# Layer 3's weight tables in float32r from high and low parts, with a reordered prologue

## What is computed

```python
x = x + conv1d(x, W, groups=4, taps=9, pad=4) + (cond @ c_weight.T + bias)[:, :, None]
for n in (1, 2, 3):
    h = gelu(cond @ W0 + b0); h = gelu(h @ W1 + b1)
    att = softmax(h @ W2 + b2)                       # 8 weights per sample
    agg_w = einsum('bk,koi->boi', att, weight)       # a 64x64 matrix per sample
    x = x + einsum('boi,bih->boh', agg_w, x) + (att @ bias_k)[:, :, None]
```

## Time and profile before

| what | value |
|---|---|
| median of three runs | 327.9 us |
| the profiled execution | 329.1 us |
| its span in the trace | 327.3 us |
| PE busy | 317.1 us (97%), 1479 instructions |
| PEld busy | 256.4 us (78%) |
| DVE busy | 253.0 us (77%) |
| ACT busy | 227.6 us (70%) |
| POOL busy | 158.8 us (49%) |
| DMA | 104.80 MB, 320 GB/s on average |

### The profile page before, as it was taken

One profiled execution on the slowest core, in us unless ns is written; L12 is line 12 of the kernel. 1 busy time (PEld: TensorE's weight loads), 2 busy tenths in 40 slices (PEclk: granted clock), 3 DMA queues, 4 the chain that ended last, 5 costly groups with the idle time before them and its releaser, 6 DMA issues.

```text
span 327.3 us, 5950 instructions
## 1 busy us (share of the span) xinstructions
PE 317.1 (97%) x1479; PEld 256.4 (78%) x1479; DVE 253.0 (77%) x231; ACT 227.6 (70%) x344; POOL 158.8 (49%) x269
## 2 busy tenths in 40 slices
PE   8899999999999999999999999999999999999993
PEld 8787868888888787688788887777888887888862
DVE  4593968788886886977888867788788878887674
ACT  5445597777777778776767777787777676777662
POOL 8001289887444454545544445555555454444500
PEclk9999999999999999999999999999999999999999
DMA  7994356998999999989998999998999999897658
GB/s 255 262 289 172 132 208 222 356 375 354 349 332 348 362 334 364 345 322 359 371 355 335 339 338 354 336 373 340 341 365 366 346 357 365 320 353 291 267 212 340
DMA packets 29948, 104.80 MB, mean 320 GB/s; under 512 B 3353, under 2 KB 3609, under 8 KB 21978
## 3 DMA queue, kind: packets, MB, share of 16 engines
q1 hardware_dynamic: 29940, 104.70, 86.2%
HBM read 36.53 MB, written 33.55 MB: 214 GB/s over the span
## 4 chain that ended last, share of the span: by engine, by line
PE 76%; DMA 8%; issue 6%; DVE 6%; ACT 2%; POOL 1%; DVEq 0%; POOLq 0%
PE bank L394 43%; PE bank L430 8%; DMA ybuf<-conv_sb 8%; PE bank L432 7%; PE bank L431 7%; PE bank L402 4%; PE bank L509 2%; DVE mix_lo L739 1%; ACT conv_sb L594 1%; PE bank L438 1%; PE bank L451 1%; POOL a_dup L359 1%; DVE ybuf L729 1%; DVE x_lo L715 1%; ACT x_hi L587 1%
## 5 line engine op out<-in xcount | busy, mean ns | idle before, releaser
L349 POOL COPY a_diag<-table 64x64 f32 (+1 forms) x128 | 87.7, 685 | 117.6 <-PE bank L402 85.1
L594 ACT ACTIVATE conv_sb<-bank 128x512 f32<-128x512 f32 x128 | 76.6, 598 | 70.6 <-PE bank L394 66.3
L715 DVE TENSOR_TENSOR x_lo<-x_sb,x_hi 128x2064 fp32r<-128x2064 f32 x32 | 74.0, 2312 | 41.6 <-ACT x_hi L587 40.4
L394 PE MATMUL bank<-x_hi,toep_hi 128*128 128x512 f32 x256 | 84.5, 412 | 0.0
L394 PE MATMUL bank<-x_lo,toep_hi 128*128 128x512 f32 x256 | 80.7, 397 | 0.0
L394 PE MATMUL bank<-x_hi,toep_lo 128*128 128x512 f32 x256 | 80.5, 396 | 0.0
L359 POOL COPY a_dup<-table 64x128 f32 (+1 forms) x128 | 64.4, 503 | 30.8 <-DVE table L803 13.2
L729 DVE TENSOR_TENSOR ybuf<-ybuf 128x2048 fp32r<-128x2048 f32 x31 | 72.1, 2324 | 1.7 <-ACT ybuf L598 1.6
L614 ACT ACTIVATE out_sb<-bank,beta 128x512 f32<-128x512 f32 x93 | 63.7, 687 | 4.6 <-PE bank L432 1.6
L587 ACT ACTIVATE x_hi<-x_sb 128x2064 fp32r<-128x2064 f32 x32 | 61.6, 1924 | 3.1 <-DMA x_sb<-in_x 2.9
L394 PEld LDWEIGHTS bank<-x_hi,toep_lo 128*128 128x128 f32 x256 | 48.3, 189 | 12.0
(11 more groups left out here) (83 smaller groups left out, 172.9 us busy)
## 6 DMA issues: line engine op xcount, KB each, us to landing
x_sb<-in_x SPq DMA_DIRECT2D x32, 1032.0 KB, 7.5
ybuf<-conv_sb SPq DMA_DIRECT2D x128, 256.0 KB, 4.5
out<-out_sb SPq DMA_DIRECT2D x30, 1024.0 KB, 7.7
out_sb<-conv_sb SPq DMA_DIRECT2D x4, 256.0 KB
out<-out_sb SPq DMA_DIRECT2D x4, 256.0 KB, 3.0
out<-x_sb SPq DMA_DIRECT2D x4, 256.0 KB, 3.3
early<-in_pairs SPq DMA_DIRECT2D x1, 640.0 KB, 4.6
x_sb<-in_toep SPq DMA_DIRECT2D x1, 640.0 KB, 6.1
```

Of the source, the lines that this page charges most:

```text
L349: nc.gpsimd.tensor_copy(a3_diag[rows, par, :, C * h + NH * e:C * h + NH * e + NH], table[0][C * e:C * e + C, here, h, :]).then_inc(comp_in, 1)
L394: last = mm(o, w[:, d, g, :], v[:, par, g, :, d:d + J], start=i + d == 0, stop=i + d == 3)
L594: nc.scalar.activation(conv_sb[:, par, g, :], conv_ps[g % banks][:, :], ACT.Copy).then_inc(conv_out, 1)
L715: nc.vector.tensor_tensor(x_lo[:, par].rearrange("p g s j -> p (g s j)"), x_sb[:, par].rearrange("p g s j -> p (g s j)"), x_hi[:, par].rea ...
```

## The change

Layer 3's tables are computed in float32r. Its eight matrices are split into a high and a low part, and so are its coefficients. The rows stand as follows: the high parts of the matrices in rows 0, 4, ... 28 and again in 32 to 60, the low parts in 64 to 92 and again in 96 to 124, the identity in row 2; against them stand the coefficients high, low, high, low, and a 1. `mrow3` lies in `ybuf[:, 1]` and no longer in `table[1]`. The eight matrices are loaded as 128 rows of 1 KB into a stage in `conv_sb[:, 0]`, the identity as 16 rows; DVE rounds and subtracts there, ahead of its memset; SP then spreads them by four DMAs (128 KB each, 1 KB pieces) and one of 16 KB, ahead of x's first load. `coef_t` becomes two tiles, filled by two copies. ACT takes tables 0, 2, 3, 4, 6, 7 and 8, 10, 12, 14. The orders of PE, ACT and DVE in the prologue change as the diff says.

```diff
-ACT_TAKES = (0, 2, 4, 6, 8, 10, 12, 14)
+ACT_TAKES = (0, 2, 3, 4, 6, 7, 8, 10, 12, 14)
+EYE = 2
+QK = 16
-        t_bank = (bank[4], bank[6], bank[7], bank[2], bank[3])
+        t_bank = (bank[4], bank[6], bank[7], bank[3], bank[2])
-        coef_t = sb("coef_t", [128, NT, B])
+        coef_t = (sb("coef_t3", [128, B], F32R), sb("coef_t21", [128, B]))
-        mrow = [table[1][:].rearrange("p b h c -> p (b h c)"), out_sb[:].rearrange("p q s n -> p (q s n)")]
+        mrow3 = ybuf[:, 1].rearrange("p t n -> p (t n)")[:, 0:C * C]
+        mrow = [mrow3.bitcast(F32), out_sb[:].rearrange("p q s n -> p (q s n)")]
+        stage = conv_sb[:, 0].rearrange("p g n -> p (g n)").rearrange("p (t n) -> p t n", n=C * C // QK)
+        w3, eye3, w3_lo = stage[:, 0], stage[0:QK, 1], stage[:, 4].bitcast(F32R)
+        w3_hi, eye3_hi = stage[:, 2].bitcast(F32R), stage[0:QK, 3].bitcast(F32R)
SP, behind row:
+            sp.dma_start(w3, own_h[0:K].rearrange("k (q n) -> (k q) n", q=QK)).then_inc(w3_in, 16)
+            sp.dma_start(eye3, own_h[K:K + 1].rearrange("o (q n) -> (o q) n", q=QK)).then_inc(w3_in, 16)
SP, behind ident:
             sp.wait_ge(rows3_zero, 1)
-            sp.dma_start(mrow[0][0:RS * K + 1:RS], own_h[0:K + 1]).then_inc(rows3_in, 16)
+            sp.wait_ge(w3_hi_set, 2)
+            sp.wait_ge(w3_lo_set, 1)
+            for part in range(4):
+                sp.dma_start(mrow[0][32 * part:32 * part + RS * K:RS].rearrange("k (q n) -> k q n", q=QK),
+                             (w3_hi, w3_lo)[part // 2].bitcast(F32)).then_inc(rows3_in, 16)
+            sp.dma_start(mrow[0][EYE:EYE + 1].rearrange("o (q n) -> o q n", q=QK), eye3_hi.bitcast(F32)).then_inc(rows3_in, 16)
             load(0, 0)
POOL:
-            for t, at in enumerate((RS * K, OWN + RS * 2 * K)):
+            for t, at in enumerate((EYE, OWN + RS * 2 * K)):
PE:
-            stream(3)
-            for g in range(4):
-                pair_products(g)
-
+            stream(2)
+            pair_products(0)
+            pair_products(1)
             pe.wait_ge(kept_in, 16)
             pe.wait_ge(coef_zero, 3)
-            pe.wait_ge(coef_set, 4)
+            pe.wait_ge(coef_set, 5)
             for t in range(NT):
                 last = nc.tensor.transpose(bank[3][:, B * t:B * t + B], coef[:, t], ident[:])
             last.then_inc(coef_t_ps, 1)
+            pair_products(2)
...
-                    pe.wait_ge(rows3_in, 16)
+                    pe.wait_ge(rows3_in, 16 * 5)
...
-                if t == 3:
+                if t == 4:
                     pe.wait_ge(c0_set, 2)
                 if t == TG:
+                    pe.wait_ge(coef_t_set, 2)
...
-                    last = mm(t_bank[t % TB][:, B * i:B * i + B], mrow[n][:, at:at + 2 * C], coef_t[:, n, :],
+                    last = mm(t_bank[t % TB][:, B * i:B * i + B], (mrow3, mrow[1])[n][:, at:at + 2 * C], coef_t[n][:],
                               start=True, stop=True)
...
             tables(0)
+            pair_products(3)
+            tables(1)
             mm(bank[1][:, 0:C], cond, cw, start=True, stop=False)
             mm(bank[1][:, 0:C], ones[:], frow, start=False, stop=True).then_inc(c0_ps, 1)
             mm(bank[2][0:C, 0:B], cw, cond, start=True, stop=True).then_inc(c0_ps, 1)
-            tables(1)
             tables(2)
ACT:
+            table_bank(0)
             x_high(0, 0, 0)
-            for t in ACT_TAKES:
-                if t < TG:
-                    table_bank(t)
+            table_bank(2)
+            table_bank(3)
+            table_bank(4)
+            table_bank(6)
+            table_bank(7)
             conv_copy(0, 0, 0, 0, banks=2)
             vcol_copy(0)
             conv_copy(0, 0, 0, 1, banks=2)
+            x_high(1, 0, 1)
             conv_copy(0, 0, 0, 2, banks=2)
             conv_copy(0, 0, 0, 3, banks=2)
             vcol_copy(1)
-            x_high(1, 0, 1)
-            for t in ACT_TAKES:
-                if t >= TG:
-                    table_bank(t)
             x_high(2, 1, 0)
+            table_bank(8)
+            table_bank(10)
+            y_high(0, 0, 0)
+            table_bank(12)
+            table_bank(14)
             conv_copy(1, 0, 1, 0, banks=2)
             conv_copy(1, 0, 1, 1, banks=2)
-            y_high(0, 0, 0)
DVE:
             nc.vector.memset(blank[:], 0.0).then_inc(blank_set, 1)
+            dve.wait_ge(w3_in, 32)
+            nc.vector.tensor_copy(w3_hi, w3).then_inc(w3_hi_set, 1)
+            nc.vector.tensor_copy(eye3_hi, eye3).then_inc(w3_hi_set, 1)
+            dve.wait_ge(w3_hi_set, 1)
+            nc.vector.tensor_tensor(w3_lo, w3, w3_hi.bitcast(F32), ALU.subtract).then_inc(w3_lo_set, 1)
             nc.vector.memset(mrow[1], 0.0).then_inc(rows21_zero, 1)
...
-            nc.vector.tensor_copy(coef_own[:, 0, 0:K, 0], att[:, 2, :]).then_inc(coef_set, 1)
+            parts = coef[:, 0].rearrange("b (w c k r) -> b w c k r", w=2, c=2, r=RS)
+            of_3 = att[:, 2, :].rearrange("b (o k) -> b o k", o=1).to_broadcast([B, 2, K])
+            nc.vector.tensor_copy(parts[:, :, 0, :, 0].bitcast(F32R), of_3).then_inc(coef_set, 1)
+            dve.wait_ge(coef_set, 4)
+            nc.vector.tensor_tensor(parts[:, :, 1, :, 0], of_3, parts[:, :, 0, :, 0], ALU.subtract).then_inc(coef_set, 1)
```

More of the change, by code:

```diff
@@ L186, in cond_resid_kernel @@
         rows3_in, rows21_in = sem("rows3_in"), sem("rows21_in")
+        w3_in, w3_hi_set, w3_lo_set = sem("w3_in"), sem("w3_hi_set"), sem("w3_lo_set")
         rows3_zero, rows21_zero = sem("rows3_zero"), sem("rows21_zero")
@@ L803, in table_bank @@
                 nc.vector.tensor_copy(dst, src).then_inc(tab_dve, 1)
-            product_copy(2)
-            product_copy(3)
-            dve.wait_ge(coef_t_ps, 1)
-            nc.vector.tensor_copy(coef_t[:], bank[3][:, 0:NT * B].rearrange("r (t b) -> r t b", t=NT)).then_inc(coef_t_set, 1)
             dve.wait_ge(toep_in, 16)
@@ L812, in _ @@
             nc.vector.tensor_tensor(taps, taps, eyes.to_broadcast([128, 2, G, 128]), ALU.add).then_inc(toep_set, 1)
+            dve.wait_ge(coef_t_ps, 1)
+            for t in range(NT):
+                nc.vector.tensor_copy(coef_t[t][:], bank[3][:, B * t:B * t + B]).then_inc(coef_t_set, 1)
+            product_copy(2)
+            product_copy(3)
+            dve.wait_ge(toep_hi_set, 1)
+            nc.vector.tensor_tensor(toep_lo[:].rearrange("p d g m -> p (d g m)"), toep,
+                                    toep_hi[:].rearrange("p d g m -> p (d g m)").bitcast(F32),
+                                    ALU.subtract).then_inc(toep_lo_set, 1)
             dve.wait_ge(c0_ps, 2)
@@ L817, in _ @@
             table_bank(1)
-            dve.wait_ge(toep_hi_set, 1)
-            nc.vector.tensor_tensor(toep_lo[:].rearrange("p d g m -> p (d g m)"), toep,
-                                    toep_hi[:].rearrange("p d g m -> p (d g m)").bitcast(F32),
-                                    ALU.subtract).then_inc(toep_lo_set, 1)
-            table_bank(3)
             x_low(0, 0)
@@ L825, in _ @@
             bias_sum(0)
-            table_bank(7)
             bias_sum(1)
@@ L829, in _ @@
             table_bank(9)
+            x_low(2, 0)
+            table_bank(11)
+            table_bank(13)
+            y_low(0, 0)
+            table_bank(15)
             bias_sum(2)
-            for t in (11, 13, 15):
-                table_bank(t)
-            x_low(2, 0)
-            y_low(0, 0)
             mix_low(0, 0)
```

## The result

The kernel after takes 334.31 us (median of 6 executions, 330.26 to 337.91), the kernel before in the same session 328.08 (327.47 to 328.58). The ratio is 1.0145, interval 1.0110 to 1.0181: slower by about 1.5%, where 326.2 us was forecast and 328.4 was the upper end of the range. Ratios here leave out executions more than 1.5% above the fastest of their kernel, and medians don't, so the medians here lie further apart, by 1.9%. The profiled execution after took 333.45 us with a span of 331.7, against 329.1 and 327.3 before.

What follows compares the result with a forecast made beforehand. The prediction took TensorE's matmuls to bound the loop, with time moving by the first mix's start. Work of -3.9 us and waits of -2.4 and +4.5 gave -1.7: 327.9 to 326.2 us, range 325.4 to 328.4.

Steps and rivals of the forecast that it cites:

- What bounds the kernel: Whole kernel: matmuls set the loop, which the change leaves alone; time moves with the first mix start, 46.38 to 44.7.
- Work taken from PE: Layer 3's tables: 32 float32r matmuls at 0.111 us replace 64 instructions, 3.6 us less; one warm-up matmul, 0.26, goes too.
- The rival that it is no cheaper: Layer 3's tables: narrow float32r matmuls cost 0.235 us each, mix at 46.65, 328.2 us; chance 0.2.
- The staged load and VectorE: Before the tables: load lands at 5.3, VectorE's split takes 0.8, memset ends at 9.5, PE idles 1.5 us before the transposes.
- The spreading and what is behind it: Loads before tables and first convolution: spreading lands at 11.8, at no cost; x near 14.7, mixrow near 17.0.
- The slower rival: Before the tables: spreading transfers starve them at 75 GB/s, first table 16.2, mix 48.2, 329.7 us; chance 0.1.
- The clock: PE's new gaps: a gap of 1.0 us left it at 1.00; a fall in a new gap would prove the forecast wrong.
- wait at the bias turn: After the first convolution group: PE waits 1.4 us for VectorE's bias sum, going on at 22.75 against 24.07 before.
- Behind the bias product: First convolution to first mix: convolution at 19.9, composition at 41.2, GpSimd's four copies in 1.35 us, mix at 44.7.
- the rule of the prediction: GpSimd's copies beside bias sum 2: only VectorE instructions with two SBUF inputs lock GpSimd out; otherwise 1.2 gain, not 1.7.
- the starved case: Before the tables: they wait for spreading data below about 100 GB/s; +1.8 us at the mix, 329.7 us, chance 0.1.
- Late load: Before the tables: staged load lands near 7.05, adding 1.75 us along the chain, 327.9 us; chance 0.12.

Runs made afterwards that it cites:

- experiment 7: Kernel after with VectorE's memset first, mixrow ahead of the spreading, one spreading transfer instead of four: 327.69 us, ratio 0.9951; with float32 tables 1.0011.
- experiment 6: Kernel after with VectorE's memset first and GpSimd's last two memsets moved behind VectorE's split: 335.41 us, ratio 1.0219.
- experiment 1: Kernel after with VectorE's memset moved back before its wait for the staged load: 335.21 us, ratio 1.0178.
- experiment 5: Kernel after with mixrow issued ahead of the spreading: 331.31 us, ratio 1.0074; with VectorE's memset first as well 1.0126; with 18 warm-up matmuls instead 1.0018.
- experiment 8: Kernel after with layer 3 in float32, rows loaded directly, no split or spreading, new orders kept: 328.10 us, ratio 1.0005; mixrow issued first as well: 1.0001.
- both moves: Kernel after with VectorE's memset first and mixrow ahead of the spreading: 333.80 us, ratio 1.0126; the same with float32 tables 333.24 us, 1.0157.
- experiment 2: Kernel after with 18 warm-up matmuls before the transposes: 335.79 us, ratio 1.0202; with all four pair products there instead: 335.49 us, 1.0207.
- experiment 3: Kernel after with VectorE's memset first and layer 3's tables in float32: 333.25 us, ratio 1.0113.

## Why the prediction was wrong

**What bounds the kernel: right.** All of the change is in the start of the first mix: 5.0 us later there, 4.4 on the span.

**Work taken from PE: right in size.** The narrow float32r matmul stands 0.111 apart at the full clock, as taken (experiment 7). The rival that it is no cheaper (0.2) is out. What is missing is that the price holds at the full clock only; it was 0.23 on average where the clock was mostly at the lower level.

**The staged load and VectorE: too early by 2.8 us.** The load landed at 6.07, not 5.3; between the load and the memset stood 0.3 for the first cast where 1.39 was needed (experiment 6), and the 0.80 of idle before the memset, which the earlier trace rows show, was not carried along. The memset ended at 12.3, not 9.5, and the gap in PE was 4.3, not 1.5. By itself this term decides nothing (experiment 1, and experiment 5 with the memset first as well): take it away, and the tables wait for the spreading instead.

**The spreading and what is behind it: the step that failed.** The working put the transfers "before 13.1, so at no cost", x at 14.7 and mixrow at 17.0, the very time at which the bias product wanted it. The four transfers were issued from 8.1, not from 6.2, and took 0.69 each on SP, not 0.62; x's load went out at 11.57, not at 9.1. It then landed at 19.5, 7.9 us later, where the working had 14.7, 5.6 later: that came from bytes divided by a rate, while a landing of 7.4 for this very load stood in the earlier trace rows. Mixrow landed at 22.3, not at 17.0. In the working's own terms 2.5 of these 5.3 us are the later issue of x, 2.3 x's longer way, and 0.5 mixrow's own; that is bookkeeping, and experiment 6 shows that the parts don't simply add. The working did follow the queue, but its mixrow had some 6 us from issue to landing, where the trace shows 8.9, and 11.1 even with the order alone (experiment 8), and it left no slack. The transfers themselves took about as long as taken: 5.5 us from the first issue to the first table's start in experiment 1 (8.1 to 13.64), 5.6 in the working (6.2 to 11.8). Experiments 5 and 7 show the step: mixrow alone moved ahead gives back 0.7%, and with both moves one transfer in place of four turns a loss (1.0126) into a gain (0.9951).

**The slower rival** had the right direction, and nearly the times: first table 16.2 (16.17), x 19.0 (19.5), mixrow 21.3 (22.3). Its chance of 0.1 was too small, and its mix at 48.2 was 3.1 too early, because it ran the rest at the full clock. Its mechanism was only half right. It had the tables wait for the spreading; in the kernel after they waited for the coefficients, behind the gap on VectorE, and x and mixrow were what the transfers made late. That its first table came at the right time was luck.

**The clock: named as what would make it wrong, and left without a price.** The text said that a gap of 1.0 had left the clock at 1.00; the gap was 4.3, and the second low stretch came after the bias product. Its 3.1 + 0.35 us come on top of the 5.3 of the late mixrow; the 1.4 us that the working had for a wait at the bias turn is not needed then, nor are 0.4 of its smaller waits (0.2 before the convolution, and 0.6 in step 1's where the trace has 0.43). 5.3 + 3.45 - 1.4 - 0.4 = 7.0 stands against the 6.7 between the mix forecast (1.7 earlier) and the mix found (5.0 later). The Trainium skill ("TensorE: Matmul & The Clock Gate", "HAM oscillation — how this bites in real kernels") says that waits for transfers can put the clock back to its lower level again and again. Experiments 1 and 2 agree with that, where the clock fell within waits of 5.7 and 3.2 us; the fall of the kernel after at 23.4, with PE idle for 0.26 only since 14.4, is not in it.

**Behind the bias product** the working stands: the wait at the bias turn is 1.0 where the path is clear (forecast 1.4), GpSimd's first four copies took 1.35, as taken:

```profile
45.10 1.35 POOL L376 COPY a_dup<-table 64x128 f32<-64x128 f32 x4 [16.47 <-DVE table L835]
```

Bias sum 2 ran beside them on VectorE (44.90 to 46.68), and the trace agrees with the rule of the prediction that it does not hold them up.

**The range** ended at 328.4 since it left out the starved case, and no case had its costs added. Late load, late split, slow queue and lower clock came together here, and the first three follow one another on one chain.

**What stays open.** Why x's load and mixrow need 7.9 and 8.9 us in the kernel after is not shown: how much is the queue, how much the shared engines. In seven kernels mixrow took 8.5 to 11.1 us when issued behind other loads. What makes the clock fall while PE is busy, and why it tends to stay low for longer with float32r tables, is open too. A spreading into 16 outer pieces and a queue of its own for mixrow were not tried. No version that leaves nothing out was measured faster than the kernel before; the nearest are experiment 5 with warm-up matmuls (1.0018) and the new order alone (1.0005).

## What to carry to other kernels

A step that moves work off the bound engine must be costed on the queue that feeds it: list every load that stands behind each new wait and each new issue, and give each the landing time that its own row shows, not bytes over a rate; where a load then lands just when it is wanted, count its slack as nothing. Transfers that fan data into a few partitions cost 0.69 us of issue each here and kept the DMA share at 0.50 while alone, so issue what is needed soonest ahead of them, and remember that this delays them in turn (3.8 us in experiment 5). And a wait of PE of several microseconds has to be priced with the clock after it.

## What the runs showed that was not expected

- Float32r matmuls with 128 moving columns: 0.111 us apart at the full clock, 0.23 where it was mostly at the lower level. In two pairs of kernels (experiments 1 and 3, and both moves with either type) the clock came back some 6 and 11 us later with them than with float32 ones; in the first pair the wait in front was longer too (5.7 against 1.8). In that pair the version with more work on PE was 2.0 us faster, in the second the two were even.
- Four transfers inside SBUF into 8 rows each: 0.69 us of SP per issue, and a DMA share of 0.50 while they are alone.
- A 256-column cast on VectorE took from 1.2 to 2.3 us beside memsets on GpSimd, and 0.29 without them.
- Eighteen idle matmuls in a gap of 4 us did nothing while a transfer was late behind it (1.0145 and 1.0202), and took the ratio from 1.0074 to 1.0018 once it was not.
